# A graph stack on one core: first sums in other PSUM banks, GpSimd's first power ahead of two reductions, and aggregation steps moved ahead of four late stages

## What is computed

```python
h = relu(layernorm(x)); x = x + attention(h, adj)    # 4 heads, softmax over the neighbours
h = relu(layernorm(x)); x = x + h @ W_self + (adj @ h / deg) @ W_neigh
h = relu(layernorm(x)); x = x + gru(relu((adj @ h) @ W_msg.T + b_msg), h)
h = relu(layernorm(x)); x = x + hyperbolic(h, adj)   # exp/log maps, tanh and artanh of row norms
```

## Time and profile before

| what | us |
|---|---|
| three runs: median, lowest, highest | 601.5, 601.31, 602.59 |
| the profiled execution, its time as a run | 602.1 |
| span from its first to its last instruction | 600.3 |

### The profile page before, as it was taken

How to read it: one execution, slowest core, us unless ns; L and a number is a source line. 1 busy time by engine, 2 the same in 40 slices (tenths; PEclk the granted TensorE clock), 3 DMA queues, 4 the chain that set the end, 5 groups by cost and what they waited for, 6 DMA issues and landing times.

```text
span 600.3 us, 12084 instructions
## 1 busy us (share of the span) xinstructions
PE 560.5 (93%) x4535; PEld 351.5 (59%) x4535; DVE 338.8 (56%) x1483; ACT 211.4 (35%) x580; POOL 100.1 (17%) x104
## 2 busy tenths in 40 slices
PE   4679899999999999999999999999999999999981
PEld 3578799999994544444444545554554444555540
DVE  4882372333323563333314687788779763676876
ACT  4530011100011110000032478778778555532433
POOL 3870100000000010000001112212122210330322
PEclk9979999999999999999999999999999999999996
DMA  8999999999940000000000001100100020110000
GB/s 230 108 108 108 106 109 108 108 108 108 109 44 4 5 14 0 1 0 1 19 0 19 18 26 30 36 13 25 36 1 20 17 86 3 36 55 36 18 36 35
DMA packets 23897, 29.17 MB, mean 49 GB/s; under 512 B 11296, under 2 KB 11936, under 8 KB 23840
## 3 DMA queue, kind: packets, MB, share of 16 engines
q0 software_dynamic: 8704, 16.78, 27.8%
q1 hardware_dynamic: 15136, 11.62, 6.4%
HBM read 72.43 MB, written 4.19 MB: 128 GB/s over the span
## 4 chain that ended last, share of the span: by engine, by line
PE 82%; DVE 10%; issue 3%; POOL 1%; ACT 1%; DMA 1%; SPq 0%; DVEq 0%; POOLq 0%
PE acc L1565 50%; PE acc L1375 9%; PE acc L1376 9%; PE acc L1405 4%; PE acc L1412 3%; PE acc L1395 1%; PE acc L1463 1%; PE acc L1462 1%; PE acc L1461 1%; DMA x<-x_rows 1%; POOL rs L1029 1%; PE acc L1497 1%; DVE hs_a L372 1%; PE acc L1468 1%; DVE mean L414 1%
## 5 line engine op out<-in xcount | busy, mean ns | idle before, releaser
L1565 PE MATMUL acc<-adj,hs_a 128*128 128x512 fp8e4 x1024 | 227.7, 379 | 2.8 <-DVE hs_a L561 2.0
L1565 PEld LDWEIGHTS acc<-adj,hs_a 128*128 128x128 f16 x1024 | 99.3, 98 | 116.7 <-DVE hs_a L561 2.2
L1375 PE MATMUL acc<-region_op,adj 128*128 128x133 f16 x1024 | 127.1, 224 | 5.0 <-issue 3.6
L1376 PE MATMUL acc<-region_op,adj 128*128 128x132 f16 x1024 | 127.2, 223 | 0.0
L1565 PE MATMUL acc<-adj,region_op 128*128 128x512 fp8e4 x512 | 118.3, 379 | 0.0
L1375 PEld LDWEIGHTS acc<-region_op,adj 128*128 128x128 fp8e4 x1024 | 100.9, 99 | 6.5 <-issue 3.7
L1376 PEld LDWEIGHTS acc<-region_op,adj 128*128 128x128 fp8e4 x1024 | 100.8, 98 | 0.1
L1565 PEld LDWEIGHTS acc<-adj,region_op 128*128 128x128 f16 x512 | 49.3, 98 | 56.7 <-issue 4.0
L1029 POOL TENSOR_TENSOR region_st<-region_st,small 128x4 f32<-128x4 f32 (+1 forms) x39 | 44.9, 1151 | 204.3 <-ACT w L1167 131.3
L1029 POOL TENSOR_TENSOR rs<-rs,small 128x4 f32 (+3 forms) x27 | 30.9, 1147 | 267.9 <-DVE rs L389 251.4
L1146 ACT ACTIVATE hs_a<-rowbuf 128x512 f32 (+1 forms) x8 | 5.0, 630 | 117.3 <-DVE rowbuf L395 117.3
(11 more groups left out here) (239 smaller groups left out, 682.7 us busy)
## 6 DMA issues: line engine op xcount, KB each, us to landing
adj<-adj_pieces POOLq DMA_DIRECT2D x32, 512.0 KB, 66.2
p_rows<-rowbuf SPq DMA_DIRECT2D x8, 256.0 KB, 2.0
region_op<-p_rows SPq DMA_DIRECT2D x8, 256.0 KB, 3.1
out_rows<-x SPq DMA_DIRECT2D x7, 256.0 KB, 2.0
x<-x_rows SPq DMA_DIRECT2D x3, 512.0 KB, 7.6
region_st<-matrices SPq DMA_DIRECT2D x1, 768.0 KB, 9.8
x<-x_rows SPq DMA_DIRECT2D x2, 256.0 KB, 4.4
hT<-region_op SPq DMA_TRANSPOSE x32, 2.3
```

Of the source, the lines that this page charges most:

```text
L1375: mm(bank[TG + it % TG][:, 0:HI], adj8[:, it, jt, :], op0[:, jt, 0:HI], start=(jt == 0), stop=False)
L1376: last = mm(bank[TG + it % TG][:, 0:LO], adj8[:, it, jt, :], op0[:, jt, HI:OPW], start=False, stop=(jt == NT - 1))
L1565: last = mm(dst, hs[:, jt, part, :], adj8[:, c * TG:(c + 1) * TG, jt, :], start=(k == 0), stop=(k == 2 * NT - 1))
```

## The change

Four edits.

1. The first four row tiles accumulate in banks 0 to 3, and DVE reads them from there for group 0. PE's wait for `acc_read` ahead of tile 4 is gone. Ahead of each eight steps of `aggregate(0, ...)`, from tile 8 on, a wait for the first `acc_read` is added, since stage 0 writes bank 0.
2. POOL's power for group 0 goes ahead of the two reductions over the partitions; the loop over the groups then begins at 1.
3. At the junction of layers three and four, six steps of `SECOND` go ahead of `update_back`, and six steps of `THIRD` go behind `new_transposes`, between it and `own_part`.
4. In stage `FOURTH + 4`, the last, `norms` and `bottom` of the stage before go from k = 8 and 14 to k = 14 and 20.

```diff
@@ attend, DVE
-                sums = acc[:, TG:2 * TG, :]
+                sums = acc[:, 0:TG, :] if isinstance(g, int) and g == 0 else acc[:, TG:2 * TG, :]
@@ gpsimd
             for it in range(AHEAD, NT):
                 fetch(it)
+            inverse_deviation(0, 0)
             pool.wait_ge(S["spread_ready"], 1)
             q.partition_all_reduce(extall[:, 4:9], ext[:, 4:9], P, bass.bass_isa.ReduceOp.max).then_inc(S["spreadall_ready"], 1)
             pool.wait_ge(S["top_ready"], 1)
             q.partition_all_reduce(topall, top, P, bass.bass_isa.ReduceOp.max).then_inc(S["topall_ready"], 1)
-            with pool.Fori(0, NG) as g:
+            with pool.Fori(1, NG) as g:
                 inverse_deviation(g, 0)
@@ attend, PE
+                dst = bank[it] if it < FIRST_TILES else bank[TG + it % TG]
                 for jt in jts:
-                    mm(bank[TG + it % TG][:, 0:HI], adj8[:, it, jt, :], op0[:, jt, 0:HI], start=(jt == 0), stop=False)
-                    last = mm(bank[TG + it % TG][:, 0:LO], adj8[:, it, jt, :], op0[:, jt, HI:OPW], start=False,
+                    mm(dst[:, 0:HI], adj8[:, it, jt, :], op0[:, jt, 0:HI], start=(jt == 0), stop=False)
+                    last = mm(dst[:, 0:LO], adj8[:, it, jt, :], op0[:, jt, HI:OPW], start=False,
                               stop=(jt == NT - 1))
@@ ball_steps
-                          FOURTH + 4: {8: (norms, FOURTH + 3), 14: (bottom, FOURTH + 3)}}
+                          FOURTH + 4: {14: (norms, FOURTH + 3), 20: (bottom, FOURTH + 3)}}
@@ tensor
                 if it % TG == 0:
                     if it >= 2 * TG:
+                        pe.wait_ge(S["acc_read"], 1)
                         aggregate(0, 2 * it - 4 * TG, 2 * it - 2 * TG)
-                    pe.wait_ge(S["acc_read"], it // TG)
+                        pe.wait_ge(S["acc_read"], it // TG)
@@ tensor, the junction of layers three and four
             embed(FIRST - 2)
+            aggregate(SECOND, 0, 6)
             update_back(FIRST - 1)
-            aggregate(SECOND, 0, 40)
+            aggregate(SECOND, 6, 40)
             aggregate(THIRD, 0, 11)
             aggregate(FIRST, 36, 40)
-            aggregate(THIRD, 11, 26)
+            aggregate(THIRD, 11, 20)
             new_transposes(FIRST - 1)
+            aggregate(THIRD, 20, 26)
             own_part(FIRST - 1)
```

## The result

The changed kernel takes 606.8 us, the median of eight runs (604.63 to 609.95), against 601.45 us for the kernel before beside it (eight runs, 600.65 to 603.29). The ratio is 1.0087, with a 95% interval from 1.0066 to 1.0107: 5.3 us slower. The forecast was 607.3 us. The profiled execution's span is 605.0 us, against 600.3.

The account below looks back on a forecast made before the run. PE, busy 93% of the span, was taken as the bound. 600.3 + 7.4 + 1.6 - 2.2 - 1.0 = 606.1 us, 5.8 more; added to the median of 601.5 this gave 607.3 us, range 604.5 to 609.5.

Parts of the forecast that it names:

- the 11.4 us: Layer one, POOL: changing back from reductions to powers delays group 1's power until 81.2 us, 11.4 us after its MODIFY_POOL_CONFIG.
- The other bound of the prediction, 9.4: POOL's change of work taken as 9.4 us instead of 11.4, giving a kernel time of 605.3 us.
- The weights: Layer one, first `own_self` at tile 11: weights ready at 90.5 us, PE waits 10.8 us and goes on 7.4 us later.
- The clock: PE behind the wait at the first `own_self`: granted clock falls to a half, costing 1.6 us.
- The bound of 3.3: Upper bound in us for the cost of PE's clock fall, twice the low stretch; the lower bound was 0.
- The lead of 3.4 us: Layer one, PE: waits of 1.4 us at tile 4 and 2.0 us ahead of tile 8 go, then the weights' wait swallows the lead.
- The late moves: Edits 3 and 4: 2.2 us won at the junction of layers three and four, 1.0 us in the last stage.
- (a): Rival, POOL in layer one: the change back is shorter or begins earlier; 602.9 or 601.9 us; chance 0.11.
- (b): Rival, POOL in layer one: the change back doesn't fall on group 1 at all, so faster, 595.9 us; chance 0.11.
- (c): Rival: the late moves don't pay, a wait reappears at `hs_ready` or in DVE's chain; 610.5 us; chance 0.04.

Follow-up runs that it names:

- the early change back: The change plus a POOL power of four constants into unused columns, behind the two reductions and ahead of the loop; 602.83 us, ratio 1.0019.
- the left-out reductions: The change with POOL's two reductions over the partitions replaced by a subtraction and an addition of the same shapes, result not the reference's; 595.61 us, ratio 0.9897.
- quiet DMA engines: The change with POOL's old order and a constants power behind the reductions, plus an unneeded reduction and power behind layer one's powers loop; 596.42 us.

## Why the prediction was right, and where its terms were off

**Where the 11.4 us go.** That POOL's change back would move from group 0 to group 1, and start only behind group 1's `ve_ready`, is what the trace of the change shows (69.5, against 69.8 forecast), and the early change back and the left-out reductions show it as a cause. Its length was mis-sized: 10.1 us, where the sum took 11.4 from the one execution that it had. Over the executions of these kernels it lay between 9.4 and 11.4 us, so the row was at the upper end. The other bound of the prediction, 9.4, is the lower end, but by chance: it was the price of the other direction.

**The weights.** From L395 to L588 it is 8.2 us as forecast. PE's first `own_self` is 5.9 us later than before, forecast 7.4: 1.3 us of the difference are the change back, and the rest goes with this trace beginning 0.3 us closer to its work (DVE reads group 0's sums at 50.13 instead of 50.46).

**The clock** was forecast to cost 1.6 us, from the one fall in the trace of before; it cost 2.5 (96.39 - 87.97 = 8.4 of lag behind tile 11, less the 5.9). The step that was off is taking the length of low clock after the resumption from one event: 3.5 us there, 5.4 here. The bound of 3.3 held.

**The lead of 3.4 us** was made (tile 8's aggregation begins 4.0 us earlier, of which 0.3 are the earlier begin of this trace, so 3.7) and swallowed by the wait, as forecast. Neither edit makes it alone. With the banks and without the moved power PE has nothing of it. With the moved power and without the banks the wait ahead of tile 8 is gone and the one at tile 4 still there, 1.3 us: tile 8's aggregation begins at 67.86, 1.5 us earlier than before in a trace that runs 0.6 us later (group 0's sums are read at 51.10), so some 2 us of the lead.

**The late moves.** The lag falls from 8.2 us (the product ahead of the six steps begins at 471.51, before it began at 463.33) to 5.8 behind the junction, 2.4 us, forecast 2.2; the last stage gives 1.1, forecast 1.0, held by DVE's L1012, not by PE. The forecast left a rest of waiting of 0.1 us at each place; the trace shows none.

**The sum.** 5.9 + 2.5 - 2.4 - 1.1 = 4.9 us, and the spans differ by 4.7; the forecast was 7.4 + 1.6 - 3.2 = 5.8. The two large terms were off in opposite directions, by 1.5 and 0.9 us, so that the total is closer than its parts is in part luck. The path, the wait and its place were right.

**The rivals.** (a), a change back that begins earlier, isn't what this order does, but it is what an added power makes it do: the forecast for that rival was 602.9, and the kernel that does it took 602.8. That they agree so closely is chance: the rival had the weights at 86.1 and PE 3.0 us late, and in the trace they are there at 83.9 and PE is 0.9 us late, with 1.8 us for the clock; the span of that execution is 599.5, the median of its runs higher. (b), no change back at all, was forecast at 595.9, with 2.4 us of the lead left by `adj`; without the reductions it is 595.6, with tile 30 waiting for its DMA. (c) didn't happen.

**The figure of the Trainium skill.** The page of the Trainium skill that the prediction named, "GPSIMD Engine Reference", gives about 6 us (5.95) for the gap behind MODIFY_POOL_CONFIG, in its section "Instruction dispatch". With quiet DMA engines the one execution shows 5.9 us into the reduction, as the Trainium skill has it, and 7.2 back, which is more. While `adj` was coming at some 108 GB/s the runs show 6.8 to 9.7 us into the reductions and 9.4 to 11.4 back, and these decided here.

## What to carry to other kernels

Before an instruction of GpSimd is moved past another, look in its queue for what the compiler puts between the two kinds of work: the price belongs to the first instruction behind the change, and whoever is moved away from that place leaves it to the next. Where the change can't be avoided, put it where nobody waits, ahead of a wait and not behind it; an instruction without use can hold that place (606.8 us became 602.8 by it). A wait that is removed on one engine shows only as much as the next one leaves: here the weights had 0.4 us of cover, and the fetch of `adj` 2.4.

## What the runs showed of the hardware

- GpSimd's change back from the reductions to the powers took 9.4 to 11.4 us in ten executions while `adj` was being fetched, and 7.2 us in the one place where the DMA engines were quiet; that the load is the reason isn't shown.
- The profile has the same 23897 DMA packets for the kernel without a change of work between reductions and powers and for the one with four.
- A wait of 3.3 us on PE was enough, in one execution of the change without the moved power, for the granted clock to be at a half for some 3.3 us, of which 2.8 lay behind the wait, when PE was working again. In the kernel before a wait of 2.0 us at the same place wasn't followed by it.
- After 9.8 us without work PE ran at 1.2 GHz for another 5.4 us; after the idle time at 26 to 33 us of the kernel before it was 3.5. In the change the clock was low for 10.2 us in all, in the two kernels with waits of 5.0 and 6.4 us for 6.8. The fall came 4.9 us after PE had stopped in the change, 4.7 us in the kernel with the first `own_self` behind tile 11, and 2.1 us in the one with the early change back.
- With matmuls of no use in the place of the wait the clock stayed at 1.00, and from `own_self` to DVE's next reading of sums it took 2.5 us less in the trace, though the weights came only 0.4 us earlier; the kernel's time was 1.8 us lower.
